# A graph attention layer in eight batches: the work ahead of and in the first rows laid in another order

## The reference

```python
h = relu(layernorm(x))                     # x: (8, 1024, 256)
q, k, v = h @ Wq + bq, h @ Wk + bk, h @ Wv + bv      # 8 heads of 32
scores = q @ k.T / sqrt(32) + (1 - adj) * -1e9       # adj: (1024, 1024), one for all
out = softmax(scores) @ v
return x + out @ Wo + bo
```

## Time and profile before

| what | before |
|---|---|
| runs | 1118.05, 1121.21, 1121.3 us; median 1121.21 |
| profiled execution | 1122.66 us, its span 1120.3 us |
| PE busy | 1099.7 us (98%) |
| ACT busy | 996.7 us (89%) |
| DVE busy | 960.2 us (86%) |
| POOL busy | 313.0 us (28%) |
| mean granted TensorE clock | 0.991 |

### The profile page before, as it was taken

One profiled execution on the slowest core, in us unless ns is written; L12 is line 12 of the kernel. 1 busy time (PEld: TensorE's weight loads), 2 busy tenths in 40 slices (PEclk: granted clock), 3 DMA queues, 4 the chain that ended last, 5 costly groups with the idle time before them and its releaser, 6 DMA issues.

```text
span 1120.3 us, 28439 instructions
## 1 busy us (share of the span) xinstructions
PE 1099.7 (98%) x10736; PEld 890.5 (79%) x10736; DVE 960.2 (86%) x1800; ACT 996.7 (89%) x1833; POOL 313.0 (28%) x505
## 2 busy tenths in 40 slices
PE   8889999999999999999999999999999999999998
PEld 6677877887878888887887877888877888878776
DVE  4778889988889888998889988898889989888886
ACT  2779999999999999999999999999999999999985
POOL 5364122142123222142112422124122142122122
PEclk9889999999999999999999999999999999999999
DMA  6842352423524244342434335243352423424211
GB/s 185 254 112 62 79 136 69 111 67 95 144 67 106 61 122 118 73 108 68 118 96 103 85 77 141 68 111 81 82 139 75 106 71 95 104 67 105 55 30 49
DMA packets 88474, 109.08 MB, mean 97 GB/s; under 512 B 24772, under 2 KB 50628, under 8 KB 88340
## 3 DMA queue, kind: packets, MB, share of 16 engines
q1 hardware_dynamic: 77188, 95.95, 31.5%
q0 software_dynamic: 10960, 11.07, 5.0%
q10 hardware_dynamic: 192, 0.26, 0.1%
HBM read 30.54 MB, written 9.44 MB: 36 GB/s over the span
## 4 chain that ended last, share of the span: by engine, by line
issue 51%; DMA 29%; POOL 15%; SPq 2%; DVE 1%; PE 1%; ACT 0%; POOLq 0%; ACTq 0%; DVEq 0%
DMA inv_rows<-inv_turned 15%; DMA inv_t<-inv_rows 14%; POOL inv_t L469 9%; POOL xn L434 3%; SPq L308 2%; POOL ln_t L419 1%; POOL mask L476 1%; DMA xn<-in_x 0%; PE ps_turn L805 0%; POOL res L439 0%; POOL ln_neg_mean L416 0%; DMA q_stack<-q_lo 0%; POOL ln_var L417 0%; POOL ln_t L423 0%; POOL ln_t L421 0%
## 5 line engine op out<-in xcount | busy, mean ns | idle before, releaser
L590 DVE CUSTOM_DVE_ANT_0 rows<-ps_scores,mask 128x1024 f32<-128x1024 f32 x512 | 615.6, 1217 | 37.0 <-PE ps_scores L765 31.6
L501 ACT ACTIVATE rows<-rows,row_min 128x1024 f32<-128x1024 f32 x512 | 589.7, 1159 | 4.6 <-DVE row_min L590 4.6
L798 PE MATMUL ps_turn<-ident_r,rows_raw 128*128 128x128 f32 x4096 | 466.5, 258 | 10.0 <-ACT turned_a L506 6.5
L798 PEld LDWEIGHTS ps_turn<-ident_r,rows_raw 128*128 128x128 f32 x4096 | 401.6, 141 | 85.5 <-ACT rows L501 25.7
L506 ACT ACTIVATE turned_a<-ps_turn 128x512 f32<-128x512 f32 x512 | 307.7, 601 | 89.5 <-PE ps_turn L798 89.4
L765 PE MATMUL ps_scores<-k_stack,q_stack 128*128 128x512 f32 x1016 | 330.2, 425 | 0.9 <-DVE row_min L590 0.9
L597 DVE COPY turned_b<-ps_turn 128x512 f32<-128x512 f32 x314 | 216.3, 689 | 85.8 <-PE ps_turn L798 80.7
L460 POOL DMA_DIRECT2D inv_rows<-inv_turned x64 | 46.4, 725 | 622.9 <-DVE inv_turned L631 617.5
L469 POOL DMA_DIRECT2D inv_t<-inv_rows x252 | 133.3, 536 | 144.0 <-DMA inv_rows<-inv_turned 139.6
L765 PEld LDWEIGHTS ps_scores<-k_stack,q_stack 128*128 128x128 f32 x1016 | 160.1, 189 | 16.8 <-DVE row_min L590 6.3
L849 PE MATMUL ps_heads<-turned_a,v 128*32 128x256 f32 x2016 | 121.8, 382 | 0.0
(11 more groups left out here) (96 smaller groups left out, 602.4 us busy)
## 6 DMA issues: line engine op xcount, KB each, us to landing
q_stack<-q_hi SPq DMA_DIRECT2D x248, 64.0 KB, 2.0
q_stack<-q_lo SPq DMA_DIRECT2D x248, 64.0 KB, 2.1
k_stack<-k_hi SPq DMA_DIRECT2D x242, 64.0 KB, 2.0
k_stack<-k_lo SPq DMA_DIRECT2D x242, 64.0 KB, 2.0
res<-in_x SPq DMA_DIRECT2D x32, 256.0 KB, 2.7
inv_t<-inv_rows POOLq DMA_DIRECT2D x252, 32.0 KB, 2.3
out<-res SPq DMA_DIRECT2D x31, 256.0 KB, 2.8
xn<-in_x SPq DMA_DIRECT2D x30, 256.0 KB, 3.1
```

The lines of the kernel that those rows point to most:

```text
L501: nc.scalar.activation(rows[:, k, :], rows[:, k, :], ACT.Exp, bias=row_min[:, k:k + 1], scale=-1.0, accum_out=row_sum[:, u % 2, j:j + 1]). ...
L590: nc.vector.tensor_tensor_reduce(out=rows[:, k, :], in0=ps_scores[n % 2][:], in1=mask[:, qt, :], scale=1.0, scalar=START_MIN, op0=ALU.add, ...
L798: tr = nc.tensor.transpose(ps_turn[half][:, k, :].bitcast(F32R), rows_raw[:, n % RING, kt * P:(kt + 1) * P], ident_r[:])
```

## The change

Tables and code of the front and of the first unit (rows 0 to 7) are rewritten. Rows 8 on use the same tables as before, except that the first phase has a step table of its own.

- **Roots.** In batch 0 ACT takes the inverse root (`Abs_reciprocal_sqrt`) of the variances, DVE does the Newton step (`first_deviations`), half by half, each half right behind its moments. POOL has no part in it. ACT loads the table of that function at the start and Exp's table behind the last copy of h.
- **Loads.** Wq stands ahead of the second half of x, the columns bq and bk are issued by ACT, Wv comes after mask tile 1, mask tile 2 is loaded early too.
- **Front on PE.** `WARM` goes from 20 to 16. Rows 0 and 1 are split: their products with the first keys (`keys` 0) and with the rest (`keys` 1) follow `qk` 3, then come `qk` 2 and rows 2 and 3. `qk` 2 has the bank `ps_heads`. The `v` steps leave the front.
- **Stacks.** POOL stacks q step 0 for heads 0 to 2, all of k step 3 and all of q step 2 (44 DMAs, before 24); SP stacks q step 0 for head 3 and k step 1 (20 before the mask load, before 20 and then 16 more). ACT issues none.
- **Rows 0 to 7.** `v` 0 goes to rows 1 and 2, `v` 1 to rows 3 to 5, `qk` 0 of the next phase to rows 6 and 7, `qk` 1 to rows 9 to 11. ACT does its exp last in a slot and copies both halves in rows 0, 3 and 6; PE runs four rows ahead, DVE three, ACT two.
- **Masks last.** SP loads mask tile 3 and the next batch's x after row 7's scores, and tiles 4 to 7 only once q step 2 is stacked.

```diff
+FIRST_STEPS = (("first_v", 0, (1, 1, 2, 2)), ("first_v", 1, (3, 4, 4, 5)), ("qk", 0, (6, 7, 7, 7)),
+               ("qk", 1, (9, 10, 11, 11)), ("qk", 2, (13, 13, 14, 14)), ("qk", 3, (17, 18, 19, 19)),
+               ("v", 0, (25, 26, 27, 27)), ("v", 1, (28, 29, 30, 30)))
+FIRST_SCORES, FIRST_MASKS, FIRST_EXPS = 4, 3, 2
+FIRST_ACT_COPIES = (0, 3, 6)
...
-WARM = 20
-MASKS_EARLY, MASKS_LATE = 2, 4
+WARM = 16
+MASKS_EARLY, MASKS_LATE = 3, 4
...
@@ sync @@
+            load_weights(sp, "q", Wq, q_weights_in)
             sp.dma_start(xn[:, PARTS:TILES, :], x_v[0, :, PARTS:TILES, :]).then_inc(x_in, 16)
+            load_weights(sp, "k", Wk, k_weights_in)
             load_mask(0, 0, 1)
+            load_weights(sp, "o", Wo, o_weights_in)
+            load_column(sp, "v", bv, o_weights_in)
+            sp.dma_start(bo_row[:], bo.partition_broadcast(P)).then_inc(o_weights_in, 16)
+            load_mask(1, 1, 2)
+            load_weights(sp, "v", Wv, v_weights_in)
+            load_mask(2, 2, 3)
+            sp.wait_ge(lo_done, START_QK.index(0) + 1)
+            stack_step(sp, 0, 0, start_stacked, range(PARTS - SP_Q_HEADS, PARTS), high=start_hi, low=start_lo)
             sp.wait_ge(lo_done, START_QK.index(1) + 1)
             stack_step(sp, 0, 1, start_stacked, high=start_hi, low=start_lo)
+            sp.wait_ge(scores_done, 2 * PARTS)
+            load_mask(MASKS_EARLY, MASKS_EARLY, MASKS_LATE)
             for piece in range(X_PIECES):
                 load_x(1, piece)
+            for h in range(PARTS):
+                sp.wait_ge(half_stacked[h], STEP_DMAS * 16)
+            for u in range(2):
+                load_mask(MASKS_EARLY + 1 + u, MASKS_LATE + 2 * u, MASKS_LATE + 2 * u + 2)
...
@@ gpsimd @@
-            deviations(1, slice(0, PARTS), PARTS)
-            deviations(1 + LN_STEPS, slice(PARTS, TILES), TILES)
             pool.wait_ge(lo_done, START_QK.index(0) + 1)
-            stack_step(pool, 0, 0, pool_stacked, high=start_hi, low=start_lo)
+            stack_step(pool, 0, 0, pool_stacked, range(PARTS - SP_Q_HEADS), high=start_hi, low=start_lo)
             pool.wait_ge(lo_done, START_QK.index(3) + 1)
-            stack_step(pool, 0, 3, pool_stacked, range(ACT_HEADS, PARTS - SP_HEADS))
+            stack_step(pool, 0, 3, pool_stacked)
+            pool.wait_ge(lo_done, START_QK.index(2) + 1)
+            stack_step(pool, 0, 2, half_stacked)
...
@@ vector @@
+            def first_deviations(half, tiles):
...
+                nc.vector.tensor_scalar(neg_mean, mean, -1.0, None, ALU.mult).then_inc(first_chain, 1)
+                dve.wait_ge(first_roots, half + 1)
+                nc.vector.tensor_tensor(t1, t0, t0, ALU.mult).then_inc(first_chain, 1)
...
+            first_low_part(2)
+            first_mask(1)
+            for n in range(2):
                 mask_row(n)
-            copy_v(0, 0, 1, V_BANKS[1])
+            first_mask(2)
+            for n in range(2, FIRST_MASKS):
+                mask_row(n)
+            first_low_part(3)
...
@@ tensor @@
+            pe.wait_ge(lo_done, START_QK.index(3) + 1)
+            pe.wait_ge(v_weights_in, 16)
...
+                if k == 0 and half == 0:
+                    pe.wait_ge(lo_done, QK_STEPS)
+                    pe.wait_ge(v_ready, V_STEPS)
```

More of the change, by code:

```diff
@@ L103, in steps @@
         return LAST_STEPS
-    return [(kind, s, at) for kind, s, at in STEPS[g] if not (first and g == 0 and kind == "o")]
+    return FIRST_STEPS if first and g == 0 else STEPS[g]
 def side_work(g, i, first, last):
@@ L211, in gnn_kernel @@
         pool_stacked = [sem(f"pool_stacked{h}") for h in range(PARTS)]
+        half_stacked = [sem(f"half_stacked{h}") for h in range(PARTS)]
         out_stored = sem("out_stored")
@@ L254, in unit, with reach @@
             return b * BATCH_UNITS + (g * UNITS + u)
-        def reach(ahead, n):
-            return range(n + ahead[(n - 1) % UNIT_ROWS], min(n + ahead[n % UNIT_ROWS] + 1, BATCH * BATCH_ROWS))
+        def reach(ahead, first_ahead, n):
+            before, here = (first_ahead if m < UNIT_ROWS - 1 else ahead[m % UNIT_ROWS] for m in (n - 1, n))
+            return range(n + before, min(n + here + 1, BATCH * BATCH_ROWS))
         def step_ended(b, g, i):
@@ L541, in _ @@
                     copy_ht(0, s, HT_BANKS[s % 2])
+                    if s == DCH - 1:
+                        first_root(1)
+                    elif s == HT_STEPS - 1:
+                        nc.scalar.activation(table_col[:], eps_col[:], ACT.Exp).then_inc(table_ready, 1)
                 elif kind == "qk":
-                    act.wait_ge(weights_ready, 2)
+                    if s % 2 == 0:
+                        act.wait_ge(weights_ready, 2)
+                    else:
+                        act.wait_ge(k_weights_in, 2 * 16)
                     k = START_QK.index(s)
-                    high_part(k + 1, 0, s, (start_hi + hi)[s][:], QK_BANKS[k % 2])
-                elif (kind, s) == ("rows", 0):
-                    act.wait_ge(lo_done, START_QK.index(3) + 1)
-                    stack_step(act, 0, 3, start_stacked, range(ACT_HEADS))
-                    for n in range(EXP_AHEAD[-1]):
-                        exp(n)
+                    if k == len(START_QK) - 1:
+                        for n in range(FIRST_EXPS):
+                            exp(n)
+                    high_part(k + 1, 0, s, (start_hi + hi)[s][:], QK_BANKS[k])
             def slot(b, g, i, first, last):
@@ L652, in take @@
                     copy_v(nb, ng, s)
+                elif kind == "first_v":
+                    copy_v(0, 0, s)
                 elif kind == "o":
@@ L682, in _ @@
-            copy_v(0, 0, 0, V_BANKS[0])
-            for n in range(2, MASK_AHEAD[-1]):
+            for half in range(2):
+                tiles = slice(half * PARTS, (half + 1) * PARTS)
+                for t in range(half * PARTS, (half + 1) * PARTS):
+                    moments(0, t)
+                first_deviations(half, tiles)
+                for t in range(half * PARTS, (half + 1) * PARTS):
+                    nc.vector.tensor_scalar(xn[:, t, :], xn[:, t, :], ln["neg_mean"][:, t:t + 1],
+                                            ln["rstd"][:, t:t + 1], ALU.add, ALU.mult).then_inc(normed, 1)
@@ L734, in side_free @@
                 if before is None:
[L735 removed]
+                    pe.wait_ge(ht_done, HT_STEPS)
                     return
@@ L909, in slot @@
                 turn(b, g, i, 1)
-                if row(b, g, i) == 0:
-                    for m in range(PARTS, SCORES_AHEAD[-1]):
-                        scores(m)
-                for m in reach(SCORES_AHEAD, row(b, g, i)):
+                for m in reach(SCORES_AHEAD, FIRST_SCORES, row(b, g, i)):
                     scores(m)
@@ L938, in slot @@
                         values(1 - g, s, piece)
+                    elif kind == "first_v":
+                        values(0, s, piece)
                     else:
```

217 lines of the change are left out of this document (119 added, 98 removed).

## The result

| | before | changed |
|---|---|---|
| runs of the first comparison | 1118.05 to 1121.30, median 1119.99 us | 1114.04 to 1115.58, median 1114.66 us |
| ratio | | 0.9947, 95% interval 0.9931 to 0.9963 |
| profiled execution, span | 1122.66, 1120.3 | 1114.08, 1112.0 |
| TensorE's waits, 0 to 75 us, behind the warm-up | 10.8 (10.5 by the earlier trace rows, and 0.3 for "issue" in the earlier trace rows) | 7.1 (the eight rows below) |
| mean granted clock of the profiled execution | 0.991 | 0.998 |

The change makes the kernel 0.53% faster, 5.9 us by the ratio; two later comparisons gave 0.9960 and 0.9952. Over all runs on record the medians are 1121.2 us before and 1116.2 changed.

What follows compares the result with a forecast made beforehand. TensorE was taken as the bound: 17.5 us lost before (10.5 waits, 7.0 clock) plus 1.3 warm-up, less 10.6 lost after (8.1 waits, 2.5 clock), gives a gain of 8.2, to 1113.0 us; range 1108.0 to 1118.0.

Steps and rivals of the forecast that it cites:

- The steady state passes the gain on: Behind the front TensorE is busy 696.75 of 700 us, so whatever is saved in the first 75 us reaches the end in full.
- Roots: Start of batch 0: root chain on ACT and DVE takes 1.2 us; normalising starts at 7.0 instead of 9.48.
- Clock in the first projection: First q projection runs at full clock, under 2 us instead of 3.52; 3.5 would mean the clock fell.
- Table load, stacks, values: Exp's load hidden ahead of `k_hi`, counted 0; stacks just in time for rows 4 to 7, counted 0; value steps moved behind row 0.
- the calendar: New dates for the front through row 8: row 0 masked from 20.4, transposed at 24.8, row 8 at 44.8 instead of 52.44.
- Warm-up: TensorE's first matmuls: 16 instead of 20, 0.33 us each, end 1.3 us earlier, at 6.8.
- Waits after: TensorE's waits in the changed kernel's first 75 us, behind the warm-up: 8.1 us together, against 10.5 before.
- The 1.5 for late inverse sums: Rows 9 to 12: 1.5 us of waits because late mask tiles hold up the inverse sums, while x is there.
- The clock after: TensorE time lost to low clock in the changed kernel: 2.5 us, bounds 0 and 6, against 7.0 before.
- (c): Rival, stacks: POOL issues each DMA in 0.75 us, landing after 5.3; 13 us more than forecast, 1126; chance 0.06.
- (b): Rival: stacks or second-half moments 1 to 2 us late, each bringing back low clock; gain 3.8, 1117.4; chance 0.14.
- (d): Rival: second half or Wq, not the roots, bounds the start; 2.5 us of gain missing, 1115.5; 0.66 shared with the forecast.

Runs made afterwards that it cites:

- experiment 3: Changed kernel with bias columns bq and bk issued by SP and the values' copy ahead of the inversion in row 6: 1111.61 us, ratio 0.9917.
- experiment 7: Changed kernel with columns by SP, values' copy ahead of the inversion, and four more identity matmuls behind the first two transpose groups: 1114.82 us, ratio 0.9938.
- experiment 8: Changed kernel run again unaltered, as the measure for others on its chip: 1116.55 us, ratio 0.9960.
- experiment 9: Kernel before with only the roots of batch 0 moved to ScalarE and VectorE, half by half, with both table loads: 1119.68 us, ratio 0.9985.
- experiment 1: Changed kernel with bias columns bq and bk again issued by SP, each behind its weights: 1114.17 us, ratio 0.9927.
- experiment 4: Changed kernel with the roots of batch 0 back on GpSimd: 1119.06 us, ratio 0.9980.
- experiment 5: Changed kernel with the two value steps back in the front, around rows 2 and 3: 1118.66 us, ratio 0.9981.
- experiment 10: Kernel before with only the warm-up shortened, 16 matmuls instead of 20: 1121.91 us, ratio 1.0002.
- experiment 6: Changed kernel with mask tiles 4 to 7 loaded ahead of the next batch's x, without waiting for q step 2's stack: 1115.17 us, ratio 0.9947.

## Why the prediction was right, and where it was not

Faster was forecast, by 8.2 us, from a median of 1121.2 to 1113.0, in a range of 1108 to 1118. Measured: 1114.66, faster by 5.9. The direction, the range and the mechanism held; the size was 1.4 times what came. The profiled execution was to take 1114.5 and took 1114.08: that is luck, since it drew a clock of 0.998.

*The steady state passes the gain on.* It did: row 8 came 5.2 us earlier (52.44 to 47.26) with 1.9 us of `qk` 1 still to do, the waits and low stretches between 59 and 72 us went too, and the span is 8.3 us shorter. TensorE is busy 696.79 of 700 us from 400 on, and was 696.75. "In full" was too strong for what lies ahead of row 8: of the 2.0 and 2.3 us by which experiments 3 and 7 reach row 8 ahead of experiment 8, 1.0 and nothing are left in the span, taken back by waits for the inverse sums.

*Roots.* 1.2 us put down, 1.12 measured. Normalising was to start at 7.0 and started at 8.63: the step that failed here is the one never written, that x lands when it did before. The change moved two loads to ACT, and I asked when bq and bk would be there, not what they would do to x. With SP's columns normalising starts at 6.83 (experiment 9) and 6.94 (experiment 1).

*Clock in the first projection.* Full in this execution, 1.97; "under 2 us" was right here and in seven more profiles; in experiments 1, 4 and 5, and in 9 and 10 of the kernel before, the clock fell there.

*Table load, stacks, values.* Hidden, as counted. Up to row 0 every date was late by about what normalising was late by, 1.6 (VectorE masked it at 22.17, forecast 20.4; TensorE transposed it at 26.76, forecast 24.8), and no row waited for a stack: rows 4 and 5 waited for the masked row, 0.6 and 0.5, where the calendar had 0.8 and 0.6. The wait of 1.5 behind the inversion was there at 1.57. From row 0 to row 8 I had 20.0 us; it took 20.5 with a low clock of 1.6 in it, and 18.9 at full clock in experiment 8, so the calendar was 1.1 too long there, which made up for part of the late x: that row 8 came only 2.5 late is in part luck.

*Warm-up.* 1.3 us in the sum, 0.6 measured: I took 0.33 us for each matmul and an end at 6.8, and the 16 took 5.98 us and ended at 7.50 (the same 16 took 5.3 to 6.6 us in the profiles here). The term belongs in the sum, as the wait behind it is counted from the warm-up's end; but it is no gain by itself, as experiment 10 shows: what ends earlier waits longer for x.

*Waits after.* 8.1 forecast, 7.1 measured. The 1.5 for late inverse sums did not come in this profile, where they were sent 0.7 us ahead of the mask tiles. In the other profiles of this family but experiment 6 VectorE waited for them, 0.4 us (experiment 8) to 4.0 (experiment 5). Another 1.0 came just behind the 75 us, which no term had.

*The clock after.* 2.5 us put down. The profiled execution had one low stretch of about 1.7. But what decides the median is the mean over executions: a granted clock of 0.996 over 18 runs of the changed kernel and 0.9935 over 58 of before. Taken over the whole span, (1 - 0.996) x 1114 = 4.5 us and (1 - 0.9935) x 1121 = 7.3 us. This is a coarser rule than the prediction's, which counts busy time in the low stretches only: for the profiled execution of before it gives 10.1 where the stretches gave 7.0. By it the term was about 2 us too small, the largest miss of the sum.

So the sum with measured terms is 10.8 + 7.3 + 0.6 (warm-up) before, 7.1 + 4.5 after: 7.1 us. The forecast's 8.2, less 0.7 for the warm-up and 2.0 for the clock, plus 1.0 of waits after, 0.3 of the clock before and the 0.3 of "issue" that I had counted only after, is the same 7.1. Measured were 4.5 to 5.9 in three comparisons. Some 1 to 2.5 us are thus not accounted for; 0.4 of them are the waits behind 75 us, and the rule for the clock can hold the rest, but that was not tested. The two profiled executions are 8.6 us apart (1122.66 and 1114.08) and not 5.9 mostly by the clock: they drew 0.991 and 0.998, further apart than the means, and their low stretches differ by 5.3 us (7.0 and 1.7).

Of the rivals, (c), the slow pace of GpSimd's issues, did not come: the first took 0.66 us, one other 0.74, one pair 1.34 and most 0.50. (b) did not come: no stack was waited for, and the second half was normalised just ahead of its transposes (13.31 and 14.96). (d) came in another form: x bounded the start. What remains open is what makes the clock fall in one execution and not in the next with the same waits; no run here was made that could tell.

## What to carry to other kernels

Where one engine is full in the steady state, count the time that it loses ahead of it, waits and lost clock apart, and take the clock from many executions, since one profile shows one draw of it. Work of that engine is cheapest where others would make it wait: one can move it out of the front into such rows, but count it, for here it won nothing up to row 8 (experiment 5). When a front gets shorter, ask which transfer becomes the next bound: here the inverse sums. And a load that is given to another engine's queue still runs beside the first loads: ask what it delays, and what waits in the same breath (here Wq for bq) before a new part can pay.

## What the runs showed of the hardware

- The same program in one and the same comparison spread over up to 9 us, and the mean granted clock of a run goes with it only in part: for the changed kernel, experiment 8, 1111.96 us at 0.999 and 1117.61 at 0.993, but also 1117.14 at 0.997 and 1120.96 at 0.994. Over its 18 runs the correlation of time and clock is -0.63 (worked out from the record); at 0.997 alone they lie between 1113.97 and 1118.19. The same wait of 1.57 us was followed by a low clock in two of the three profiles of the changed kernel and not in the third.
- The same 16 matmuls of the warm-up took 5.34 to 6.58 us (experiments 5 and 7).
- A few hundred 4-byte elements, two columns of 1 KB each, issued by ScalarE, moved the landing of SP's 256 KB loads beside them: the first tile was read at 4.06 to 4.39 us instead of 3.44 to 3.74, the third at 5.69 to 6.30 instead of 4.53 to 4.83 (seven profiles each).
- A 16 KB transfer landed 1.8 to 2.5 us behind the end of its issue when sent just ahead of 2 MB of loads on another engine's queue, and 5.4 to 6.9 us when sent behind them (five and nine profiles).
- Two table loads of different sets in one kernel took 1.28 us each, and the next instruction started 0.02 us behind.
